# Recommendation tower on one core: which groups are split, and where the gathers stand in GpSimd's queue

## What is computed

```python
e = jnp.stack([tbl_0[ids[:, 0]], ..., tbl_38[ids[:, 38]]], axis=1)      # (512, 39, 16)
x0 = xk = e
for idx, (W, b) in enumerate(params):                                   # three layers of 128
    z = relu(jnp.einsum('bhd,bkd,hks->bsd', x0, xk, W) + b[None, :, None])
    if idx != 2: xk, direct = z[:, :64], z[:, 64:]                      # direct parts are collected
    else: direct = z
logit = jnp.sum(jnp.concatenate(direct, axis=1), axis=-1)
h = relu(jnp.concatenate([logit, dense_ctx], axis=1) @ W_top1 + b_top1)
h = relu(h @ W_top2 + b_top2)
y = h @ W_top3
```

## Time and profile before

| | |
|---|---|
| median of three runs | 642.39 us (640.81 to 642.78) |
| the profiled execution, its own time | 640.99 us |
| its span, from the first to the last instruction | 639.2 us |
| TensorE busy | 609.1 us, 1928 matmuls |
| VectorE busy | 565.2 us |
| GpSimd busy | 467.6 us |
| ScalarE busy | 285.8 us |
| DMA moved | 98.20 MB |

### The profile page before, as it was taken

The page is one execution under the profiler, slowest core; times in us unless marked ns, Lnnn a source line. Parts: engine busy times, 40 slices in busy tenths (PEclk is TensorE's granted clock), DMA queues, the critical chain, the costliest instruction groups (busy, mean ns, idle before and its releaser), DMA issues.

```text
span 639.2 us, 7209 instructions
## 1 busy us (share of the span) xinstructions
PE 609.1 (95%) x1928; PEld 363.2 (57%) x1928; DVE 565.2 (88%) x509; ACT 285.8 (45%) x341; POOL 467.6 (73%) x277
## 2 busy tenths in 40 slices
PE   0679999999999999999999999999999999999998
PEld 0235566665656566665656565665656565666553
DVE  1548999999999999999999999999999999999660
ACT  2124454545344554545344554545444554545323
POOL 6718787887878887887878888887878888707240
PEclk9979999999999999999999999999999999999999
DMA  7789787886949395877949495877949395962000
GB/s 236 178 204 205 159 192 161 185 178 154 208 108 217 78 227 117 198 152 162 202 106 218 96 220 107 197 152 161 203 112 222 88 219 106 207 138 70 2 0 0
DMA packets 28511, 98.20 MB, mean 154 GB/s; under 512 B 8081, under 2 KB 17041, under 8 KB 20434
## 3 DMA queue, kind: packets, MB, share of 16 engines
q1 hardware_dynamic: 21263, 93.39, 66.3%
q0 software_dynamic: 5120, 1.32, 1.8%
q10 hardware_dynamic: 2115, 3.36, 1.5%
HBM read 94.20 MB, written 3.84 MB: 153 GB/s over the span
## 4 chain that ended last, share of the span: by engine, by line
PE 89%; DMA 5%; POOL 3%; issue 1%; SPq 1%; ACT 0%; DVE 0%; ACTq 0%; DVEq 0%
PE z L544 44%; PE z L550 12%; PE z L552 12%; PE z L555 12%; PE z L535 4%; POOL gathered L368 3%; DMA x_rep<-x_rows 2%; DMA gathered<-in_tables,rows_sb 1%; DMA x_rows<-gathered 1%; PE z L538 1%; PE z L537 1%; PE spare L596 1%; PE z L620 1%; PE xk L620 1%; DMA base_sb<-in_base 0%
## 5 line engine op out<-in xcount | busy, mean ns | idle before, releaser
L415 DVE TENSOR_TENSOR products<-x_rep,xk 128x1024 f32<-128x1024 f32 (+1 forms) x290 | 366.5, 1323 | 29.0 <-ACT xk L646 14.4
L310 POOL TENSOR_TENSOR low<-products,high 128x1024 fp32r<-128x1024 f32 x112 | 265.6, 2390 | 101.4 <-ACT high L662 95.6
L544 PE MATMUL z<-products,w_whole 128*128 128x512 f32 x672 | 311.2, 595 | 0.0
L662 ACT ACTIVATE high<-products 128x1024 fp32r<-128x1024 f32 x176 | 184.8, 1058 | 213.3 <-DVE products L415 173.6
L368 POOL DMA_INDIRECT gathered<-in_tables,rows_sb x160 | 201.2, 1258 | 46.5 <-issue 44.8
L544 PEld LDWEIGHTS z<-products,w_whole 128*128 128x128 f32 x672 | 127.8, 190 | 111.4 <-issue 97.3
L550 PE MATMUL z<-high,w_high 128*128 128x512 f32 x352 | 183.9, 522 | 0.4 <-ACT high L662 0.4
L552 PE MATMUL z<-high,w_low 128*128 128x512 f32 x352 | 138.5, 393 | 0.0
L555 PE MATMUL z<-low,w_high 128*128 128x512 f32 x352 | 109.7, 393 | 6.3 <-DVE low L310 5.0
L310 DVE TENSOR_TENSOR low<-products,high 128x1024 fp32r<-128x1024 f32 x64 | 92.2, 1442 | 0.0
L550 PEld LDWEIGHTS z<-high,w_high 128*128 128x128 f32 x352 | 66.3, 188 | 39.1 <-issue 25.1
(11 more groups left out here) (36 smaller groups left out, 108.7 us busy)
## 6 DMA issues: line engine op xcount, KB each, us to landing
x_rep<-x_rows SPq DMA_DIRECT2D x60, 768.0 KB, 15.2
x_rep<-x_rows SPq DMA_DIRECT2D x62, 512.0 KB, 8.2
x_rows<-gathered SPq DMA_DIRECT2D x15, 225.0 KB
x_rep<-x_rows SPq DMA_DIRECT2D x8, 384.0 KB, 8.0
x_rep<-in_w ACTq DMA_DIRECT2D x2, 1280.0 KB, 9.7
gathered<-in_tables,rows_sb POOLq DMA_INDIRECT x160
x_same<-x_rows SPq DMA_DIRECT2D x15, 90.0 KB
x_same<-x_rows SPq DMA_DIRECT2D x16, 78.0 KB
```

The costliest lines, as they stand in the source:

```text
L310: ops.tensor_tensor(low[0:p, slot, 0:n, :], products[0:p, index % RING, 0:n, :], high[0:p, slot, 0:n, :].bitcast(fp32), ALU.subtract).then ...
L415: nc.vector.tensor_tensor(slots, rep, row.unsqueeze(1).broadcast_to([p, n, N]), ALU.mult).then_inc(made, 1 + pair)
L544: mm = nc.tensor.matmul(out, w_whole[0:p, at, i, :], products[0:p, slot, i, :], start=(t + i == 0), stop=(t + i == tiles[layer] - 1))
L662: nc.scalar.activation(high[0:p, slot, 0:n, :], products[0:p, index % RING, 0:n, :], ACT.Copy).then_inc(rounded, 1)
```

## The change

Group 15 of layer 2 (index 1 in its letters) stays split but its low part goes to GpSimd, group 18 becomes split with its low part on VectorE: layer 2 is now `wpwpdpwpwh`, with 4 low parts on GpSimd, one on VectorE and four whole groups; before it was `wdwpwpwpwh`, with 3, one and five. Layer 1 has the same letters in another order: `ppwwpwpddh`. Twelve of 24 groups are split, eight with low parts on GpSimd. The pair 0 and 1 is now two split groups, the pair 2 and 3 two whole ones.

The ten gathers of chunk c + 2 are issued in two bursts: nine at index 11, one at index 18, each behind the low part of that index if there is one. ScalarE's `after_layer0` goes from index 18 to 19.

```diff
-KINDS = {1: "pwppwpwddh", 0: "dwww", 2: "wdwpwpwpwh"}
+KINDS = {1: "ppwwpwpddh", 0: "dwww", 2: "wpwpdpwpwh"}
...
+GATHERS = {11: 9, 18: 1}
+assert sum(GATHERS.values()) == GB
...
-            def gather(c):
-
-                if c >= 2:
-                    pool.wait_ge(x0_written, 16 * WRITES * (c - 1))
-                for j in range(GB):
-                    row = rows_sb[:, c * GB + j:c * GB + j + 1]
-                    pool.indirect_dma_start(out=gathered[:, c % 2, j * D:(j + 1) * D], out_offset=None, in_=tables,
-                                            in_offset=bass.IndirectOffsetOnAxis(ap=row, axis=0)) \
-                        .then_inc(gather_done[c % 2], 16)
+            def gather(c, j):
+
+                row = rows_sb[:, c * GB + j:c * GB + j + 1]
+                pool.indirect_dma_start(out=gathered[:, c % 2, j * D:(j + 1) * D], out_offset=None, in_=tables,
+                                        in_offset=bass.IndirectOffsetOnAxis(ap=row, axis=0)) \
+                    .then_inc(gather_done[c % 2], 16)
 
             def body(c):
 
+                sent = 0
                 for index in range(len(BODY)):
-                    if index == N1 and c + 2 < C:
-                        gather(c + 2)
                     if BODY[index][4] == LOW_POOL and not (c == C - 1 and index in LAYER0):
                         low_part(pool, nc.gpsimd, c, index)
+                    if index in GATHERS and c + 2 < C:
+                        if sent == 0:
+                            pool.wait_ge(x0_written, 16 * WRITES * (c + 1))
+                        for j in range(sent, sent + GATHERS[index]):
+                            gather(c + 2, j)
+                        sent += GATHERS[index]
...
-            gather(0)
-            gather(1)
+            for c in range(2):
+                for j in range(GB):
+                    gather(c, j)
...
-                    if index == N1 + N0 + 4 and not last:
+                    if index == N1 + N0 + 5 and not last:
                         after_layer0(c)
```

## The result

The changed kernel takes 652.71 us (median of four runs, 651.7 to 653.21) against 641.93 us: a ratio of 1.0167, 95% interval 1.0146 to 1.0188, so it is slower by 10.8 us. The 641.93 is the median of four runs of the kernel before, where three had given 642.39. The forecast was 652.2. The profiled execution took 653.21 us, its span is 651.4.

A forecast was written before the change was run, and what follows sets the result against it. TensorE paced the old kernel at 35.89 us a turn; the GpSimd chain would make it 36.64. Fourteen turns add 10.5, two gain 0.7: + 9.8 on 642.39 gives 652.2 us, range 648 to 656.

The forecast's parts named there:

- The split group's gain: One more split group in layer 2 saves TensorE 0.34 us in each of 16 turns, 5.4 us, if operands are on time.
- The chain through GpSimd: Low parts and gathers make low part 19 0.96 us late for TensorE: a turn of 36.64 us against 35.89.
- The wait for `direct2`: ScalarE makes direct2 after group 23, ahead of rounding group 4; low part 4 starts 2.07 us after group 23 ends.
- The second chain: Layer 1's new order: low part 1 follows VectorE's chain, giving a turn of about 36.1 us by itself, under 36.64.
- After layer 0 one index later: On ScalarE it moves behind the rounding of group 18; its results are needed a dozen groups on: 0.
- the gathers' landing: Tenth gather ends 4.55 us later; x0_rep reloads still land with 2.3 us to spare before layer 0: 0.
- The sum over the turns: Turns 0 to 13 lose 0.75 us each, 10.5; turns 14 and 15 gain 0.7 together: + 9.8 us.
- GpSimd busy over 85%: Sign expected in the profile if the forecast case holds: GpSimd's busy time over 85%.
- GpSimd keeps up: Faster rival: the nine gathers need 11.1 us instead of 14.0, TensorE never waits, 637.0 us; chance 0.15.
- the tenth gather passes VectorE: Near-zero rival: it gets in ahead of low part 18, the chain is 0.81 us shorter, 644.5 us; chance 0.15.

The follow-up runs named there:

- e5_8_1_1: Changed kernel with eight gathers at index 11, one at 18, and one for the chunk after at 21: 636.48 us, ratio 0.9909 to the kernel before.
- e3_eleven_split: Changed kernel with group 18 whole again, so eleven split groups and eight low parts on GpSimd: 646.56 us, ratio 1.0078 to the kernel before.
- e2_direct2_later: Changed kernel with ScalarE's after_layer2 at index 5, so group 4 is rounded before direct2 is made: 643.97 us, ratio 1.005 to the kernel before.
- e9_9_0_1: e5_8_1_1 with nine gathers at index 11 and none at 18, still one ahead at 21: 646.88 us, ratio 1.0076 to the kernel before.
- e1_one_burst: Changed kernel with all ten gathers in one burst at index 11: 694.62 us, ratio 1.083 to the kernel before.
- e6_8_1_1_later: e5_8_1_1 with after_layer2 also moved to index 5: 638.08 us, ratio 0.9926 to the kernel before.
- e7_tenth_at_15: Changed kernel with the tenth gather at index 15 instead of 18: 692.41 us, ratio 1.0788 to the kernel before.
- e10_8_0_2: e5_8_1_1 with no gather at index 18 and two for the chunk after at 21: 643.9 us, ratio 1.0046 to the kernel before.

## Why the prediction was right

*The split group's gain* (0.34 us a turn) is there: e5_8_1_1 runs turns of 35.55, the number of that step, and ends 5.6 us under the kernel before where the step had 5.4. In the two profiled executions the difference is 4.2 (spans 639.2 and 635.0), mainly mainly since the first turn is long, so the close fit of the medians is in part luck.

*The chain through GpSimd* held link by link (table above), with a sum of 36.64 against 36.70. Against the turn of e5_8_1_1, in which no low part is late, TensorE loses 0.39 us up to the start of group 16 and 0.79 more up to that of group 20 (7.78 and 14.45 behind group 11, against 7.39 and 13.27). The step had 1.1 in all, a quarter of it at group 15; there it is a third (and the due time of low part 15 adds up to x + 23.07, not 23.09). That it was the cause and not a coincidence is shown by e3_eleven_split (take away VectorE's low part behind 17: the gather's 0.8 us goes, and the turn of 36.2 is that of the step's remainder, 36.16), by e2_direct2_later (shorten its start) and by e5_8_1_1 (shorten its burst by one gather: the whole loss goes).

*The wait for `direct2`*, the first link, is real, but it only decides while the burst is long: 8.7 us with nine gathers (652.7 to 644.0), nothing with eight.

*The second chain*, 36.1 by its own, is shown by e9_9_0_1: its turn of 36.11 and the wait for low part 1 in it.

*After layer 0 one index later* and *the gathers' landing* cost nothing: e5_8_1_1 has the first and runs at TensorE's own 35.55, and VectorE waits for x0_rep in no turn of the changed kernel. The reload of x0_rep starts 341.07 - 323.78 = 17.29 after VectorE's group 14; the step had 12.74 + 4.55 = 17.29.

*The sum over the turns* was a little short, and the total fits to 0.5 us by luck: the forecast added 9.8 where the medians differ by 10.8, to a 642.39 that came out as 641.93. In the two profiled executions 12.2 us of difference divide into 1.8 ahead of group 11 of turn 0 (66.81 against 65.02), 11.1 in fourteen turns (0.79 each, forecast 0.75), and -0.65 in the last two (forecast -0.7). The 1.8 at the start, forecast as nothing, isn't the change's: up to that point e1_one_burst, e2_direct2_later, e5_8_1_1, e6_8_1_1_later, e7_tenth_at_15, e9_9_0_1 and e10_8_0_2 run the changed kernel's own code, set-up included, and reach it at 64.96 to 65.83.

*A sign that the profile's page doesn't show* is "GpSimd busy over 85%": it has 78% of the span. In the turn from 323.53 to 360.23 alone it is 32.23 of 36.70 us, 88%.

*The rival "GpSimd keeps up"* is refuted for this kernel: the gathers were held back in the new order too, 314.28 to 328.26 being the 14.0 of before, though the delays fell on other gathers of the burst. With it falls, for this mix, the inference of the Trainium skill that VectorE's two-input operations leave a gather's descriptors alone (page "SBUF — State Buffer", section "Who interferes with whom"): the tenth gather takes 1.76 behind VectorE's low part of group 18 and 0.96 where that one is gone or comes after it.

*The rival "the tenth gather passes VectorE"* is what every second turn of e2_direct2_later does. In the changed kernel it happened in no turn: the tenth gather took 1.76 or 1.77 in all fourteen, and VectorE asked 0.7 us before low part 17 ended (332.30 against 333.00).

Where my picture was wrong is seen in e1_one_burst: I had VectorE wait for one low part. The forecast didn't suffer, since the change itself puts a gather behind low part 17.

## What to carry to other kernels

When work moves to a helper engine, its busy share (78% of the span here, 88% of a turn) says little. Write its queue down for one turn, with the due time of every item, and look for the longest stretch that nothing can break up; here one gather of 1.25 us moved out of a burst was worth 16 us of 650. Where two engines hold each other back, look at which requests fall inside the other's busy stretch, and leave a gap in a row of helper instructions where the main engine will ask: 0.2 us behind the end of a low part it found the way free, 0.7 us ahead of the end it paid, and so did the gather behind it.

## What the runs showed of the hardware that I had not expected

An instruction of VectorE with two SBUF operands that comes during a low part on GpSimd waits for the whole unbroken row of GpSimd's tensor operations: 5.38 us (e1_one_burst), 5.31 (e7_tenth_at_15) and 5.50 (turn 0 of e9_9_0_1) where one alone takes 1.22. A break in which GpSimd starts a gather, 0.16 us behind the low part, is enough to let it in (1.80 in the changed kernel), and so is one of 0.81 us in which GpSimd idles (1.76 in the later turns of e9_9_0_1). A gather that starts 0.06 us ahead of VectorE's instruction (323.82 and 323.88 in e5_8_1_1) lengthens neither.
